# Order of two sets of sixteen SyncE moves in a two-convolution residual kernel with deformable sampling

## What is computed

```python
def deform(x, w_off):                       # x: (8, 32, 128, 128)
    off = conv3x3(x, w_off).reshape(B * C, H * W, 2)
    rows = clip(off[..., 0] + row_of_pixel, 0, H - 1)
    cols = clip(off[..., 1] + column_of_pixel, 0, W - 1)
    r0, r1, c0, c1 = floor(rows), ceil(rows), floor(cols), ceil(cols)
    # bilinear mix of x at (r0, c0), (r1, c0), (r0, c1), (r1, c1), each channel with its own offsets

def group_norm(v):                          # 32 groups for 32 channels: mean and variance per channel

att = softmax(attention) @ depthwise3x3(group_norm(x))
x = x + softmax(global_attention) @ (pointwise @ att)
x = x + conv3x3(deform(group_norm(x), w_off), w_conv) + b_conv
```

## Time and profile before

| | us |
|---|---|
| median of 3 runs (lowest, highest) | 739.05 (738.85, 739.9) |
| profiled execution | 740.63 |
| its span (first to last instruction) | 738.8 |
| TensorE busy, share of the span | 690.1, 93% |
| VectorE, ScalarE, GpSimd busy | 519.5, 475.7, 491.6 |
| share of the 16 DMA engines' time taken by SyncE's queue | 71% |
| mean granted TensorE clock | 0.981 |

### The profile page before, as it was taken

How to read it: one execution, slowest core, us unless ns; L and a number is a source line. 1 busy time by engine, 2 the same in 40 slices (tenths; PEclk the granted TensorE clock), 3 DMA queues, 4 the chain that set the end, 5 groups by cost and what they waited for, 6 DMA issues and landing times. The chain is left out here.

```text
span 738.8 us, 10814 instructions
## 1 busy us (share of the span) xinstructions
PE 690.1 (93%) x3500; PEld 247.4 (33%) x3500; DVE 519.5 (70%) x1031; ACT 475.7 (64%) x841; POOL 491.6 (67%) x434
## 2 busy tenths in 40 slices
PE   4799989999999889998999979999899999997966
PEld 4333333333333233333333333333333333332322
DVE  3687996598954886749955698566985595657592
ACT  7487867785675836676467654667576674876560
POOL 4004968879687486766686575857766849699650
PEclk9999989999999989999999999999999999999998
DMA  8969904999789894989959799696968563657554
GB/s 141 186 102 148 177 10 104 205 145 197 136 195 180 148 200 104 232 146 170 184 133 238 133 166 166 155 220 122 204 127 190 140 148 66 160 109 166 133 123 112
DMA packets 240878, 113.08 MB, mean 153 GB/s; under 512 B 140880, under 2 KB 235184, under 8 KB 239024
## 3 DMA queue, kind: packets, MB, share of 16 engines
q1 hardware_dynamic: 216784, 100.55, 71.0%
q10 hardware_dynamic: 24032, 11.78, 8.4%
HBM read 31.59 MB, written 16.78 MB: 65 GB/s over the span
## 5 line engine op out<-in xcount | busy, mean ns | idle before, releaser
L1317 DVE COPY_PREDICATED other_row<-down_ps,row_diff 128x768 f32<-128x768 int32 x128 | 124.4, 1024 | 139.4 <-ACT down_ps L920 139.1
L715 PE MATMUL off_ps<-x1a,wo 128*64 128x512 f32 x768 | 178.9, 601 | 2.1 <-DVE other_row L1329 2.1
L1115 POOL TENSOR_TENSOR other_row<-other_row,x_quads 128x512 f32<-128x512 f32 x64 | 76.3, 1193 | 154.2 <-DVE other_row L1329 154.2
L715 PE MATMUL off_ps<-x1b,wo 128*64 128x512 f32 x768 | 175.9, 593 | 0.0
L606 PE MATMUL c_ps<-xb,w 128*64 128x512 f32 x336 | 150.8, 598 | 5.6 <-DVE x1a L1301 5.5
L606 PE MATMUL c_ps<-mapb,w 128*64 128x512 f32 x336 | 151.7, 595 | 0.0
L608 PE MATMUL c_ps<-xa,w 128*64 128x512 f32 x336 | 150.8, 598 | 0.0
L909 ACT ACTIVATE other_row<-row_diff 128x768 f32<-128x768 f32 x128 | 101.7, 843 | 68.2 <-POOL row_diff L1101 63.0
L608 PE MATMUL c_ps<-mapa,w 128*64 128x512 f32 x294 | 132.7, 595 | 0.0
L1101 POOL TENSOR_TENSOR row_diff<-x_quads 128x594 f32<-128x594 f32 x64 | 79.5, 1243 | 43.7 <-ACT x_quads L945 43.7
L920 ACT ACTIVATE down_ps<-off_ps,bias_o 128x512 f32<-128x512 f32 x64 | 41.7, 652 | 84.1 <-PE off_ps L715 75.6
(11 more groups left out here) (134 smaller groups left out, 970.4 us busy)
## 6 DMA issues: line engine op xcount, KB each, us to landing
x1b<-x1a SPq DMA_DIRECT2D x28, 520.0 KB, 7.6
mapb<-mapa SPq DMA_DIRECT2D x28, 520.0 KB, 6.9
mapa<-mapped SPq DMA_DIRECT2D x224, 64.0 KB, 2.1
out_dram<-x1a SPq DMA_DIRECT2D x49, 256.0 KB, 4.7
x_quads<-x1a SPq DMA_DIRECT2D x192, 65.0 KB, 3.1
xb<-in_x_dram SPq DMA_DIRECT2D x48, 256.0 KB, 8.1
xa<-in_x_dram ACTq DMA_DIRECT2D x40, 256.0 KB, 6.8
xa<-in_x_dram SPq DMA_DIRECT2D x16, 256.0 KB, 6.9
```

The lines of the kernel that those rows point to most:

```text
L715: last = nc.tensor.matmul(off_ps[k % 2][64 * t:64 * t + 64, CH * n:CH * n + CH], wo[wpar][:, kx, 64 * t:64 * t + 64], rows[:, 4 * k:4 * k ...
L1115: step(pool.tensor_tensor(split(column), split(column), own, ALU.add))
L1317: last = dve.copy_predicated(other_row[n][:, :, KR // 2 * odd:KR // 2 * odd + KR // 2, :], bass.AP(tensor=rows.tensor, offset=rows.offset ...
```

## The change

Inside SyncE's loop over the images, for image i >= 1, the lower moves to mapa are issued in front of the moves of the lower quadrants. The wait for the mapped chunks and, for i >= 2, the wait for image i - 2's conv2 stand in front of both now.

```diff
                 if prev:
                     sp.wait_ge(mapped_ready, NK * i)
-                    move_quads(sp, i % 3, 1)
                     if i >= 2:
                         sp.wait_ge(conv2_done, 8 * (i - 1))
                     move_mapa(1)
+                    move_quads(sp, i % 3, 1)
                     sp.wait_ge(mapa_moved[1], A_MOVES * DMA * i)
                     copy_mapb(1)
```

## The result

| | before | after |
|---|---|---|
| median (lowest to highest), us | 739.47 (738.85 to 740.16), 4 runs | 783.82 (782.29 to 785.47), 4 runs |
| ratio, 95% interval | 1 | 1.060 (1.058 to 1.062) |
| span of the profiled execution | 738.8 | 783.7 |
| TensorE busy | 690.1 | 702.1 |
| mean granted clock | 0.981 | 0.963 |

What follows compares the result with a forecast made beforehand. TensorE, 93% busy, and an equally long 87.6 us loop through clamp and SyncE were taken as the bound. Clamp's lateness of 50.9 us less 3.0 at the end, added to 740.6, gave 788.5, so 787 for the median; range 772 to 807.

Steps and rivals of the forecast that it cites:

- Leg A: From clamp of image i to its fifth mapped chunk (k = 4): 27.7 us, 26.0 in image 1.
- Leg C: From the start of SyncE's edited block to clamp: 13.9 us before, 25.2 with the change in image 4.
- the pair: SyncE's sixteen mapa issues and sixteen lower quadrant issues together: 23.65 us in either order in image 4.
- Leg B: From the fifth mapped chunk to SyncE's edited block: 45.94 us before, 41.05 with the change, as upper quadrants issue faster.
- Lateness of clamp 7: Clamp's delay against before, summed over images 1 to 7: 50.9 us.
- The tail: After the last image's clamp: TensorE's mapb wait goes, giving back 3.0 us; the rest of its work stays as before.
- ScalarE's wait: At L941, the first instruction of clamp, waiting for quadrant moves: to grow from 22.1 us to some 60 to 70.
- Rival 1: SyncE's upper quadrants stay slow by their own transfers, so the queue gives no relief: 805 us; chance 0.13.
- Rival 2: Slack in SyncE and TensorE's reserves meet the lateness once, some 3 us an image: 750 to 770 us; chance 0.13.
- Rival 3: TensorE's 15.5 us mapb wait goes and clamp's lateness stays hidden: 723.5 us; chance 0.02.
- Rival 4: SyncE's moves queued ahead delay the quadrants by no more than a 1.6 us landing: 724 to 737 us; chance 0.02.
- Rival 5: Both sets of SyncE's moves fly and land together, so their order means nothing: 739 us; chance 0.02.

Runs made afterwards that it cites:

- Experiment 2: The change plus clamp of the lower quadrants at k = 3 instead of k = 2, against the kernel before: 734.25 us, ratio 0.993.
- experiments 4 and 10: The change in image 7 alone (4) and in images 1 to 6 only (10), against the kernel before: 747.76 us (1.010) and 774.48 us (1.046).
- experiment 6: Order of before, xb loads of images 3 to 7 cut to one row of sixteen (not computing the reference), against the kernel before: 720.72 us, ratio 0.973.
- experiment 7: The change with clamp of the lower quadrants at k = 3, ahead of ScalarE's four xa loads, against the kernel before: 736.76 us, ratio 0.994.

## Why the prediction was right, and where its terms were off

**The mechanism** held step by step. Clamp was late, everything behind it in ScalarE's order with it, SyncE waited for the fifth mapped chunk, and the lateness went round. Experiment 2 shows that it needs clamp at k = 2, experiments 4 and 10 that it adds up over the images.

**Leg A**, 27.7 us, is measured at 27.6 in images 2 to 6 (346.41 to 374.03 in image 3). In image 1 the prediction kept 26.0 us; it was 22.7 (165.45 to 188.18). This term was missed. In image 1 the conv1 groups end at k = 2, so the next x1's normalisation stands in front of chunk 3 in VectorE's order, and it was done while VectorE waited for the late clamp. The step to image 2 was +5.1 us and not +8.7: A -3.2, where nothing had been put, C +9.1 instead of +10.5, B -0.7 instead of -1.8.

**Leg C**: the pair was put at 23.65 us in image 4 and took 24.99; in image 1 it took 26.8, and landed 2.4 us after. The block began 0.6 us later as well (136.19 against 135.56), so the first step was +10.9 instead of +8.6. Why the pair and its landing took longer in image 1 stays open. This and the terms above partly cancel: after image 2 clamp was late by 16.0 instead of 17.3.

**Leg B**: 41.05 us predicted for images 3 to 4, 39.3 measured (374.03 to 413.29). The upper quadrants were right (10.5 expected, 10.5 to 11.6 measured) and so was the store's wait for conv2's seventh group: the store began 22.0 us behind the chunk, 22.6 expected. The way from the store to the block took 17.2 us, not the 18.45 of before.

**Lateness of clamp 7**: 50.9 predicted, 45.6 measured; steps 10.9, 5.1, 4.8, 5.9, 3.5, 6.2, 9.2.

**The tail** was to give 3.0 back and gave 0.7. TensorE's wait for mapb in front of L616 did go in the last image, as predicted. But chunk 5's offsets, which stand in front of it, came after a wait of 11.77 us and ran at the lower clock. These offsets in before, then in the changed kernel with the window over them:

```profile
667.11 2.80 PE L715 MATMUL off_ps<-x1a,wo 128*64 128x512 f32 x12 [2.08 <-DVE other_row L1329]
...
712.60 5.39 PE L715 MATMUL off_ps<-x1a,wo 128*64 128x512 f32 x12 [11.77 <-DVE other_row L1329]
```

```profile
712.60:718.00 5.40, 5.40 (x14) 1.70 (x16) 5.13 (x8) 3.58 (x6) 5.14 (x5) 0.50 0.82 199
```

The 24 matmuls took 8.3 us instead of 5.4, and L616 began 17.63 us behind clamp 7 in both kernels (657.61 to 675.24, 703.17 to 720.80). "What follows is TensorE's own work, as before" had left out that the same work takes longer behind a longer wait. The 0.7 us come from further differences of the same kind behind L616 (1.7 won, 1.0 lost). The steps were over by 5.3 us and the tail's relief by 2.3; the two errors point in opposite ways, and 44.9 us of span remain of the predicted 47.9. That the number came within 3 us is in part luck.

**ScalarE's wait** at L941 was put at 60 to 70 us and is 90.8. The sum for clamp itself was nearly right, but ScalarE gets there earlier: its wait for the store behind x1's first group (L865, 23.3 us in before) is 9.6 now, and its waits for TensorE's offsets at L920 fell from 75.6 to 34.7. A wait at a place grows by the lateness of what it waits for and by what its engine gains ahead of it.

**The rivals.** Rival 1 (no relief on the queue) is refuted by experiment 6. Rival 2 (the loop opens) is refuted by the changed kernel itself, whose clamps lie 91.4 to 93.5 us apart; image 4 alone shows that part of a single lateness is lost on the way, but not where each image adds its own. Rival 3 (faster) is what happens with clamp at k = 3, at a third of its size. Rival 4 (cheap issues) falls with the issue times: sixteen moves in front put clamp 1 back by 10.9 us. The rule of the Trainium skill that the prediction quotes ("DMA: Bandwidth & Descriptors", section "Anatomy of one DMA — SWDGE (gpsimd) path"), that the fixed cost of a DMA is mostly completion and issues are nearly free, does not describe these SyncE issues, which held SyncE for 0.65 us each. Rival 5 falls with the landings 1.6 us after the last issue in both orders.

The version with clamp at k = 3 and the mapa moves first is the fastest that computes the reference, 734.25 us, 0.7% below before.

## What to carry to other kernels

In an issuing engine's list the order of two sets is a choice of whose reader waits: look up both readers, and whose own list stands still meanwhile. Here the set that went first had cost its reader, TensorE, 15.5 us of waiting in all; the set that went last is read by a clamp, and behind that clamp stood work of ScalarE, VectorE and GpSimd for chunk 3, which did not need it. Moving the clamp one chunk back made the same reordering harmless. Trace the loop of waits all the way round before counting slack, since a delay on a loop without slack comes back in every round, and half of it may cost far less than half.

## What the runs showed of the hardware

TensorE's busy time rose by 12 us, for the same matmuls. The timeline of TensorE in the changed kernel behind one of its new waits, and the windows around it (start and end, length, busy us of TensorE, its weight loads, VectorE, ScalarE and GpSimd; then the granted clock):

```profile
446.03 1.11 PE L606 MATMUL c_ps<-mapb,w 128*64 128x512 f32 x1 [3.20 <-ACT x1a L868]
...
448.64 0.68 PE L606 MATMUL c_ps<-mapb,w 128*64 128x512 f32 x1
...
449.17 0.59 PE L606 MATMUL c_ps<-mapb,w 128*64 128x512 f32 x1
```

```profile
442.00:446.00 4.00, 0.83 (x4) 0.00 (x0) 2.32 (x3) 3.97 (x7) 0.28 (x1) 0.93 1.03 223
446.00:449.00 3.00, 2.97 (x8) 1.00 (x10) 2.90 (x6) 3.00 (x5) 0.62 (x1) 0.53 1.25 192
449.00:455.00 6.00, 6.00 (x30) 1.81 (x26) 5.02 (x24) 4.09 (x7) 5.76 (x6) 1.00 1.23 250
```

After 3.2 us of waiting the granted clock was at 0.53 for 3 us, nearly all of it at the lower of TensorE's two levels (1.2 GHz of 2.4), and the same matmul took 1.11 us, then 0.59 once the clock was back. The six steps of this group took 3.6 us to their last start instead of some 2.1, so the wait cost a further 1.4 us when it was over.

The length of the wait alone does not say whether this happens. In the changed kernel the clock also fell behind waits of 3.17, 3.08, 3.08 and 3.09 us (at 352.59, 376.02, 469.47 and 560.91), in three of these only from the second or third matmul on, and behind one of 2.31 us (at 259.80); behind one of 3.09 us (at 283.23) it stayed at 1.00. In the kernel before it fell behind mapb waits of 4.05, 4.13 and 2.76 us, and stayed at 1.00 behind those of 1.94 and 2.10 us. The wait at 446.03 lies in leg A, in which TensorE has no part. In leg B it has one in the changed kernel, since the store waits for conv2's seventh group; what the lower clock costs there was not separated. In the last image TensorE is on the path, and there the lower clock took the tail's relief, as shown above.

The same issues hold SyncE longer behind large transfers: sixteen quadrant moves took 10.4 us at the least and 16.1 behind the xb loads (at 529.65 of before), and one 520 KB copy to mapb or x1b took 0.6 us to issue on a free queue and up to 2.4 behind other transfers. On ScalarE four xa loads held the engine's computing up for 4.3 us in experiment 7.
